# Local attention with scaling folded into the exponent, transposed outputs, and projections from f16 parts

## The reference

```python
h = shift_token(x)                      # second half of the features from the token before
q, k, v = jnp.split(h @ wqkv, 3, -1)    # 128 x 1536, 8 heads of 64
q = l2norm(q) * qs; k = l2norm(k) * ksc
q, k = rotary_xpos(q, k)                # x*cos*scale + rotate_half(x)*sin*scale
sim = einsum('bhwid,bhwjd->bhwij', q * 8, k_of_this_and_previous_window_of_64)
sim = where(mask, -max, sim)            # a band of 65 keys
o = softmax(sim) @ v
x = x + o @ wo
```

## Time and profile before

| | us |
|---|---|
| median of 3 runs | 1677.23 |
| lowest and highest | 1675.93, 1678.6 |
| the profiled execution | 1680.32 |
| its span, first to last instruction | 1678.5 |

### The profile page before, as it was taken

One profiled execution on the slowest core, in us unless ns is written; L12 is line 12 of the kernel. 1 busy time (PEld: TensorE's weight loads), 2 busy tenths in 40 slices (PEclk: granted clock), 3 DMA queues, 4 the chain that ended last, 5 costly groups with the idle time before them and its releaser, 6 DMA issues. The chain is left out here.

```text
span 1678.5 us, 26415 instructions
## 1 busy us (share of the span) xinstructions
PE 1360.0 (81%) x9350; PEld 645.6 (38%) x9412; DVE 1211.6 (72%) x1912; ACT 875.7 (52%) x1677; POOL 887.5 (53%) x980
## 2 busy tenths in 40 slices
PE   2368989989999775775899999968779999998597
PEld 1112222222222123452555555543335555555333
DVE  6268888888888643346888888858578888888484
ACT  1126666667666563224666666633145666665422
POOL 0866766667676101115877777710087777777000
PEclk9659999999999998887999999998989999999898
DMA  3333332333333101001111111101011111000001
GB/s 90 75 57 70 58 70 58 70 65 69 70 58 70 26 1 50 1 2 36 24 24 24 24 24 24 24 1 41 13 29 24 24 24 24 22 21 22 1 0 52
DMA packets 161398, 61.14 MB, mean 36 GB/s; under 512 B 139722, under 2 KB 153076, under 8 KB 161268
## 3 DMA queue, kind: packets, MB, share of 16 engines
q1 hardware_dynamic: 161268, 59.45, 16.8%
HBM read 8.73 MB, written 2.10 MB: 6 GB/s over the span
## 5 line engine op out<-in xcount | busy, mean ns | idle before, releaser
L642 DVE TENSOR_REDUCE row_max<-max_ps 128x2 f32<-128x1024 f32 x256 | 313.0, 1223 | 73.7 <-PE max_ps L514 72.3
L673 ACT ACTIVATE prob<-scores_ps 128x1024 f32<-128x1024 f32 x256 | 262.1, 1024 | 149.3 <-PE scores_ps L494 145.9
L1628 POOL TENSOR_TENSOR la_turned<-la_raw,lw_rot 128x1024 f32<-128x1024 f32 x64 | 154.9, 2420 | 183.4 <-ACT la_raw L1533 156.9
L1285 PE MATMUL la_ring<-lw_wqkv,la_hT 128*128 128x512 f32 x384 | 200.8, 636 | 46.2 <-DVE la_hT L1402 27.4
L494 PE MATMUL scores_ps<-stack 128*128 128x512 f16 x512 | 156.2, 387 | 41.8 <-ACT prob L673 40.9
L1523 ACT ACTIVATE la_prob<-la_s,la_neg_max 128x128 f32<-128x128 f32 x512 | 156.4, 391 | 52.7 <-DVE la_neg_max L1447 52.7
L1635 POOL TENSOR_TENSOR la_turned<-la_turned,la_swapped 128x1024 f32<-128x1024 f32 x64 | 151.1, 2361 | 21.4 <-DVE la_swapped L1429 16.8
L528 PE MATMUL heads_ps<-prob,v_pad 128*32 128x512 f32 x1024 | 138.1, 612 | 1.1 <-ACT prob L673 1.1
L514 PE MATMUL max_ps<-stack 24*128 24x512 f16 x512 | 102.7, 398 | 30.0 <-DVE row_max L642 17.6
L1639 POOL TENSOR_TENSOR la_turned<-la_turned,la_inv 128x1024 f32<-128x1024 f32 x64 | 121.8, 1904 | 5.0
L494 PEld LDWEIGHTS scores_ps<-stack 128*128 128x128 f16 x512 | 34.2, 97 | 209.3 <-ACT prob L673 160.7
(11 more groups left out here) (156 smaller groups left out, 2803.3 us busy)
## 6 DMA issues: line engine op xcount, KB each, us to landing
la_v_back<-la_v_own SPq DMA_DIRECT2D x112, 130.0 KB, 2.3
X<-in_x SPq DMA_DIRECT2D x8, 256.0 KB, 5.0
stack<-stack_tok SPq DMA_TRANSPOSE x128, 3.2
out<-X SPq DMA_DIRECT2D x8, 256.0 KB, 2.5
lw_wqkv<-in_wqkv SPq DMA_DIRECT2D x2, 768.0 KB, 4.6
stack<-shift_row SPq DMA_DIRECT2D x64, 2.0 KB
lw_rot<-in_rot SPq DMA_DIRECT2D x2, 512.0 KB, 6.4
lw_w<-in_fw SPq DMA_DIRECT2D x2, 341.0 KB
```

The source lines that it names most:

```text
L642: nc.vector.tensor_reduce(row_max[:, grp % 2, w // 2, :, w % 2], max_ps[:], AX.X, ALU.max).then_inc(max_made, 1)
L673: nc.scalar.activation(prob[:, c % 4, 2 * pr:2 * pr + 2, :], scores_ps[:], ACT.Exp, scale=1.0 / LOGIT_SCALE).then_inc(exp_made, 1)
L1285: nc.tensor.matmul(ring_ps[:, r % 2, :], hT[:, b % 2, t * P:(t + 1) * P], wqkv[:, use * INNER:(use + 1) * INNER], start=True, stop=True).t ...
L1628: nc.gpsimd.tensor_tensor(spun, raw[:, T % 2].rearrange("p s (h f) -> p s h f", f=LD), rot[:, T % TPB, :, 0, :].unsqueeze(2).to_broadcast( ...
```

## The change

Only `local_attention` and its buffers are changed. Part by part:

- **Projections.** The tokens are split in two f16 parts (`h16`: ACT rounds, L1549 and L1550 of the new kernel; DVE subtracts, L1436 and L1438) and so are the weights, times 64, once a layer (`w16`). Each projection is three f16 matmuls (high by high, high by low, low by high) in place of one in f32. The copies out of `ring` divide by 64.
- **Norm of q.** POOL multiplies only k by 1/norm (512 elements). The scores are so made of q that is rotated but not divided; the maximum is multiplied by 1/norm (a new `bias`, DVE), and the exponential on ACT takes 1/norm as its scale, a value per token.
- **Softmax sum.** The exponential also gives its sum (`accum_out` to `sums`). DVE inverts the sums and multiplies the probabilities by them before they are transposed (`share`). The column of ones, `take_out` and `o_tok` go.
- **Values.** In `weigh` the values are stationary and the probabilities move, so that the output is already transposed: the four transposes of `o_tok` go, and ACT copies `o` to `oT`.
- **Order.** Each engine's slot is rewritten.

The core of the diff:

```diff
             def project(T, use):
-                nc.tensor.matmul(ring_ps[:, r % 2, :], hT[:, b % 2, t * P:(t + 1) * P],
-                                 wqkv[:, use * INNER:(use + 1) * INNER], start=True, stop=True
-                                 ).then_inc(ring_filled, 1)
+                for n, (hp, wp) in enumerate(((0, 0), (0, 1), (1, 0))):
+                    mm = nc.tensor.matmul(ring_ps[:, r % 2, :], h16[:, b % 2, hp, t * P:(t + 1) * P],
+                                          w16[:, wp, at:at + INNER], start=(n == 0), stop=(n == 2))
+                mm.then_inc(ring_filled, 1)
...
             def prob_turn(T):
-                pe.wait_ge(exp_made, T + 1)
                 for half in range(2):
+                    pe.wait_ge(shared, 2 * T + half + 1)
...
             def weigh(T, half):
-                for j in range(4):
+                for pair in (2 * half, 2 * half + 1):
                     for w in range(2):
-                        mm = nc.tensor.matmul(o_ps[64 * w:64 * w + 64, j, 0:LD + 1],
-                                              probT[:, 4 * half + j, 64 * w:64 * w + 64],
-                                              (v_back, v_own)[w][:, at, 4 * half + j, :], start=True, stop=True)
+                        for e in range(2):
+                            h = 2 * pair + e
+                            mm = nc.tensor.matmul(o_ps[64 * e:64 * e + 64, pair, 64 * w:64 * w + 64],
+                                                  (v_back, v_own)[w][:, at, h, :],
+                                                  probT[:, h, 64 * w:64 * w + 64], start=True, stop=True)
...
             # PE, slot(n): the order now
+                scores(U); [square of the sequence before]
+                transpose(R, TURN_Q); prob_turn(O); transpose(R, TURN_K)
+                weigh(O, 0); project(T, PROJ_Q); [wo]; weigh(O, 1)
+                project(T, PROJ_K); project(T, PROJ_V); [mean]
...
             def norms(T):
-                nc.vector.tensor_scalar(sumsq[:, par], sumsq[:, par], 1e-24, -0.5, ALU.max,
-                                        ALU.mult).then_inc(clip_made, 1)
+                nc.vector.scalar_tensor_tensor(out=sumsq[:, par], in0=sumsq[:, par], scalar=1e-24,
+                                               in1=minus_half[:], op0=ALU.max, op1=ALU.mult
+                                               ).then_inc(clip_made, 1)
...
             def maxima(T):
+                dve.wait_ge(max_made, T + 1)
+                dve.wait_ge(inv_made, T + 1)
+                nc.vector.tensor_tensor(bias[:, T % 2].rearrange("p (c e) -> p c e", e=2),
+                                        neg_max[:, T % 2].rearrange("p (e c) -> p c e", e=2),
+                                        inv[:, T % 4, 0:LH].rearrange("p (c e) -> p c e", e=2),
+                                        ALU.mult).then_inc(bias_made, 1)
+            def share(T):
+                par = T % 2
+                dve.wait_ge(exp_made, T + 1)
+                nc.vector.reciprocal(inv_sum[:], sums[:, par]).then_inc(inv_sum_made, 1)
+                dve.wait_ge(inv_sum_made, T + 1)
+                for half in range(2):
+                    heads = slice(4 * half, 4 * half + 4)
+                    nc.vector.tensor_tensor(prob[:, par, heads], prob[:, par, heads],
+                                            inv_sum[:, heads].unsqueeze(2).to_broadcast([P, 4, KEYS]),
+                                            ALU.mult).then_inc(shared, 1)
...
             def exps(T, heads):
                     ins = nc.scalar.activation(prob[:, T % 2, h, :], s_ps[:, place(h), :], ACT.Exp,
-                                               bias=neg_max[:, T % 2, place(h):place(h) + 1])
+                                               bias=bias[:, T % 2, h:h + 1], scale=inv[:, T % 4, h:h + 1],
+                                               accum_out=sums[:, T % 2, h:h + 1])
...
             # POOL, slot(n)
-                polish(T)
                 pool.wait_ge(plain_made, T + 1)
                 pool.wait_ge(swap_made, T + 1)
                 nc.gpsimd.tensor_tensor(turned[:, T % 2], turned[:, T % 2], swapped[:],
                                         ALU.add).then_inc(added_rot, 1)
+                polish(T)
-                heads = turned[:, T % 2].rearrange("p s (h f) -> p (s h) f", f=LD)
+                heads = turned[:, T % 2, 1].rearrange("p (h f) -> p h f", f=LD)
                 nc.gpsimd.tensor_tensor(heads, heads,
-                                        inv[:, T % 2].unsqueeze(2).to_broadcast([P, 2 * LH, LD]),
+                                        inv[:, T % 4, LH:2 * LH].unsqueeze(2).to_broadcast([P, LH, LD]),
                                         ALU.mult).then_inc(scaled, 1)
```

353 lines of the change are left out of this document (189 added, 164 removed).

## The result

| | before | after |
|---|---|---|
| median, us | 1676.58 (1674.66 to 1678.6, 4 runs) | 1725.05 (1723.38 to 1725.96, 4 runs) |
| span of the profiled execution | 1678.5 | 1723.8 |

The changed kernel is slower: ratio 1.0289, 95% interval 1.0273 to 1.0305. The forecast was 1736, its range 1632 to 1790; +59 us was forecast and +48 measured.

The account below looks back on a forecast made before the run. PE was taken to bound first, DVE and POOL close behind; after the change, a closed ring of DVE and POOL. +3.45 us a sequence times 16 is +55, plus 4 for layer starts: span 1737.5, median 1736 us, range 1632 to 1790.

Parts of the forecast that it names:

- The ring of sines, addition and `share`: DVE and POOL, each tile: these steps form a closed chain of waits, 10.0 us in place of 9.0 to 9.2.
- rival A: DVE's `share`, its second operand one repeated value, does not wait for POOL: 1631 us (1605 to 1665), chance 0.24.
- The sign that the prediction gave: In the steady stretch, DVE's two `share` products show one of 2.4 us or more beside POOL's L1685.
- Once a sequence: DVE's sines come later behind the wo product, +4.65 us; low f16 parts before a new sequence, +1.25 us.
- PE: PE per tile: transposes of o_tok go (0.80 us), three projections save 0.25 each, 8.97 to 7.42 us.
- The loop of the exponentials: ACT's exponentials with PE's projections end at 8.3 us, scores at 9.7; hidden inside the tile with 1.5 us slack.
- Rival B: ACT's exponentials bound the kernel at 0.7 us each: 11.0 us a tile, 1800 us in all, chance 0.08.
- Rival C: PE's clock falls to half for one slot in three: +43 us, 1779 us, chance 0.05.
- The upper end of the case: DVE's `bias` falls into POOL's cosines in one slot of four, 2.4 us each, 38 in all: 1774 us.
- The layers' starts and ends: Weights split before a layer's first projection, two more roundings and three more DVE products: 2.1 us a layer, +4 us.

## Why the prediction held, point by point

- **The ring of sines, addition and `share`: right.** 9.88 us for 10.0. The steps match: `share` ends 1.16 after the addition (1.17), `bias` ends 3.05 after it (3.05), the sines begin at 6.1 (6.2) and end at 7.4 (7.5). The part left for `bias` to wait on the k product, 0.63 or 0.72, is what the walk gave (0.65).
- **The repeated operand (rival A): out.** `share` stands still like any product of two SBUF operands: 2.82 for 1.29. By the Trainium skill ("SBUF — State Buffer", Who interferes with whom) it had to, as a DVE instruction with two inputs in SBUF that meets a POOL instruction reading SBUF; the trace agrees. With the inverse in PSUM the mutual holding up is gone (POOL's steps beside it 0.22 for 0.55). The sign that the prediction gave, a product of 2.4 us or more beside L1685, is there in the first slot of a sequence only; in ordinary slots the sums come too late for it.
- **Once a sequence: right.** +4.31 (14.19 - 9.88) for +4.65, and +1.21 (11.09 - 9.88) for +1.25; of the two low-part products the second, 2.73 on DVE's list, stands behind the addition.
- **PE: right in an ordinary tile.** PE is busy 6.96 us of it where it was 8.67, 1.71 less for the 1.55 forecast; over a sequence 33.74 for 38.46, 4.7 less for 6.2. None of it shows in the time. The run with f16 alone says more: its 2.8 us a sequence were worth 0.4 by themselves.
- **The loop of the exponentials: the term that was mis-sized.** The prediction had the last exponential done 5.2 us after the first began; it took 6.11. The prediction says that it takes 0.4 for an exponential, but its 8.3 is what the old 0.26 gives: from the copy of q at 5.7, three copies and four exponentials make 5.7 + 3 x 0.47 + 4 x 0.26 = 8.15, and with 0.4 it would be 8.7. Measured, an exponential is 0.44, which makes 0.7 of the 0.9 that are missing; q's copy starts 2.78 after the first exponential and not 2.6, which makes the rest. The scores come 1.8 after that and not 1.4. A slack of 1.5 us was forecast; what is left is 0.5, for the loop's own steps (6.11, 1.8, maximum and `bias` 1.4, handover 0.1) add up to 9.4. By the Trainium skill ("ScalarE: Activation LUTs", What ACT_TABLE_LOAD costs) a second operand of one value per partition adds about 93 ns; an estimate from that page's figure for the scale alone is 0.35 in place of 0.26. The trace has 0.34 to 0.36 from an ACTIVATE to its READ_ACCUMULATOR, which fits, and then 0.09 to the next ACTIVATE; no run has the scale without the sum, so how the 0.18 divide between them is not shown.
- **The seed: missing.** The walk treated the small steps on POOL as waiting only for SBUF. They also wait for ACT's seed, which stands behind the last exponential. That second ring holds 9.88 as well, less than 0.1 us under the first, so the total is right although one of two closed rings was not seen. That the unseen one is not the longer is luck: no step of the prediction kept it under 10.0. Had it not been there, the forecast would have come out the same (the run with plain exponentials: 9.88); had the first not been there, too (the run with the sines moved: 9.89, less at the sequence's end).
- **Rival B, exponentials as the bound:** in its pure form wrong (it wanted 0.55 each), but it had the right place. **Rival C, the clock:** it put +43 us on one slot in three; in the changed kernel the clock was 0.98 over 900 to 1000, and four slots of about 11.0 cost 4 us. In the version with the early seed it came in force, together with the collision.
- **The upper end of the case, `bias` falls into the cosines:** absent from the changed kernel (`bias` never takes over 0.9 us), and the main event in two of the experiments, mostly at 1.6 to 2.1 us and at most 2.32, 2.4 having been the estimate.
- **The layers' starts and ends:** -2.3 for +4. The prediction put all of the weights' splitting ahead of the first projection, on ACT and DVE; the kernel gives most of that for k and v to POOL. The first projection starts 1.3 us later than before (766.5 for 765.2), and the first maximum 0.6 earlier (787.40 for 788.03).

The forecast of the median was 11 us too high, that of the span 13.7. A sequence of 45.11 for 45.9 makes 12.6 of that (0.12 in each of four tiles, 0.34 at the end) and starts and ends make 6.3; the 4.9 us of unsteady slots, which no term of the sum had, go the other way. So a part of the closeness is errors that cancel.

## What to carry to other kernels

When the busiest engine is relieved, walk the rings of waits that remain before believing in the gain: each engine's last step in a slot and the next engine's first. List every input of each step in the ring, also the small ones (here a 16-element seed behind eight exponentials). On DVE and POOL, order decides: a DVE step with two inputs in SBUF and a POOL step that meet at a slot's border stand one behind the other, and a tiny step behind a long one loses most. A wait that holds the long one back was worth 110 us where the tiny step was caught in most tiles, and nothing where it was caught in four of 64.

## What the runs showed of the hardware

- The sum of an exponential is read out by an instruction of its own, 0.19 to 0.26 us long, with 0.09 from its start to the next ACTIVATE; with sum and scale per token the distance of two exponentials grew from 0.26 to 0.44.
- A DVE instruction with two inputs in SBUF and a POOL product go one after the other, instruction by instruction: between the halves of `share` POOL's small steps grew from 0.22 to 0.55, and an 8-element `bias` took up to 2.32 behind POOL's cosines of 2.35. Whoever comes second waits for the rest of the first, whatever its own size. A second input that is one value repeated counts like any other; with that input in PSUM POOL's steps kept their 0.22. The sum of squares, with one input in SBUF, kept its 1.20 beside the cosines (957.23, in the changed kernel).
- An f16 matmul of 512 columns lies 0.22 us from the next at a granted clock of 1.00; the f32 projection that three of them replace took 0.91.
- With PE busy 72 to 79 of 100 us the granted clock was 0.98 and 1.00 in some orders and 0.88, 0.94 and 0.95 in others, with stretches of 0.75. The same share of busy time gave different clocks (and a matmul at the lower clock is busy for longer, 620 ns for 379); what decides between them these runs don't show.
